# A two-layer model on one core: norms, FFN and query, key and value products in two halves of the tokens, a reordered mixer, and attention with rows stacked by four heads

## What is computed

```python
x = x + mamba2_mixer(layernorm(x))   # 32 heads of 64, state 128, 4 taps
x = x + ffn(layernorm(x))            # sigmoid(x w1) * (x w2), then w3; ternary weights, 704 wide
x = x + attention(layernorm(x))      # 16 heads of 16, causal, ALiBi
x = x + moe(layernorm(x))            # 64 experts, 6 per token, 64 slots each, and a shared expert
```

```python
attn = q @ k.T / sqrt(16) + slope * (j - i) + causal_mask
y = softmax(attn) @ v
```

## Time and profile before

| | |
|---|---|
| median of 3 runs | 1536.63 us (1531.63 to 1536.78) |
| the profiled execution: its own time | 1536.63 us |
| its span | 1534.8 us |
| TensorE busy | 1199.7 us, 78% |
| DVE busy | 909.1 us, 59% |
| ACT busy | 648.4 us, 42% |
| POOL busy | 584.1 us, 38% |
| DMA | 159.50 MB, mean 104 GB/s |

### The profile page before, as it was taken

How to read it: one execution, slowest core, us unless ns; L and a number is a source line. 1 busy time by engine, 2 the same in 40 slices (tenths; PEclk the granted TensorE clock), 3 DMA queues, 4 the chain that set the end, 5 groups by cost and what they waited for, 6 DMA issues and landing times.

```text
span 1534.8 us, 23644 instructions
## 1 busy us (share of the span) xinstructions
PE 1199.7 (78%) x8164; PEld 731.2 (48%) x8166; DVE 909.1 (59%) x1766; ACT 648.4 (42%) x1496; POOL 584.1 (38%) x789
## 2 busy tenths in 40 slices
PE   3799977778999876878999867779899775779950
PEld 2355544454555543555555534455555533555520
DVE  4577764446877744446977653456877643453426
ACT  3644423556444232546444224546544123431540
POOL 2255531210477712210577621110677611116660
PEclk9899988899999987998999987998999876989985
DMA  7455543400333235200333247001333529028779
GB/s 280 148 182 183 179 112 40 47 2 19 111 110 111 88 79 60 25 2 32 127 108 105 67 79 81 4 9 36 118 108 110 169 65 137 16 82 300 151 105 372
DMA packets 105957, 159.50 MB, mean 104 GB/s; under 512 B 10816, under 2 KB 67776, under 8 KB 105152
## 3 DMA queue, kind: packets, MB, share of 16 engines
q1 hardware_dynamic: 91056, 129.63, 33.1%
q0 software_dynamic: 9216, 19.98, 5.1%
q10 hardware_dynamic: 5568, 8.39, 1.5%
HBM read 104.55 MB, written 40.83 MB: 95 GB/s over the span
## 4 chain that ended last, share of the span: by engine, by line
PE 54%; DVE 14%; issue 9%; POOL 9%; ACT 6%; DMA 5%; ACTq 1%; SPq 1%; POOLq 0%; DVEq 0%
PE bank L1057 12%; PE bank L1099 5%; PE bank L982 5%; DMA joint<-pool_b 3%; PE bank L1163 3%; PE bank L1086 3%; PE bank L1078 3%; PE bank L1242 3%; DVE nmax L1668 2%; PE bank L1093 2%; DVE pool_c L1516 2%; PE bank L1184 2%; PE bank L1227 2%; DVE joint L1532 2%; PE bank L1315 2%
## 5 line engine op out<-in xcount | busy, mean ns | idle before, releaser
L1057 PE MATMUL bank<-xnT,joint 128*128 128x512 f32 x544 | 268.8, 618 | 3.4 <-ACT joint L745 1.7
L1959 POOL TENSOR_TENSOR joint<-joint 128x512 f32<-128x512 f32 x128 | 168.5, 1318 | 238.8 <-DVE joint L1532 237.6
L1516 DVE SCALAR_TENSOR_TENSOR pool_c<-bank,params,pool_c 128x511 f32<-128x511 f32 (+2 forms) x216 | 161.1, 747 | 81.1 <-ACT pool_c L706 75.7
L1668 DVE TENSOR_REDUCE nmax<-bank 128x1 f32<-128x512 f32 (+3 forms) x176 | 108.6, 638 | 112.3 <-PE bank L1204 111.2
L1057 PEld LDWEIGHTS bank<-xnT,joint 128*128 128x128 f32 x544 | 99.8, 197 | 101.8 <-issue 93.0
L982 PE MATMUL bank<-consts,pool_c 128*128 128x128 f32 (+1 forms) x368 | 69.5, 291 | 82.3 <-ACT pool_c L715 39.9
L848 ACT ACTIVATE pool_c<-bank 128x512 f32<-128x512 f32 (+1 forms) x176 | 95.0, 553 | 89.7 <-PE bank L1229 89.4
L1099 PE MATMUL bank<-wout,pool_c 128*128 128x256 f32 x512 | 127.0, 393 | 1.2 <-DVE pool_c L1557 1.2
L745 ACT ACTIVATE joint<-bank,dt_ 128x64 f32<-128x64 f32 x512 | 111.6, 338 | 13.0 <-PE bank L982 12.9
L1099 PEld LDWEIGHTS bank<-wout,pool_c 128*128 128x128 f32 x512 | 99.1, 197 | 34.3 <-issue 21.7
L731 ACT ACTIVATE pool_c<-bank 128x512 f32<-128x512 f32 x64 | 38.2, 598 | 175.6 <-PE bank L1057 175.6
(11 more groups left out here) (266 smaller groups left out, 2415.3 us busy)
## 6 DMA issues: line engine op xcount, KB each, us to landing
pool_b<-dA_rows SPq DMA_DIRECT2D x64, 256.0 KB
pool_b<-dec_rows SPq DMA_DIRECT2D x96, 128.0 KB
joint<-pool_b SPq DMA_DIRECT2D x48, 256.0 KB, 13.8
acc<-xrow SPq DMA_DIRECT2D x13, 640.0 KB, 5.3
joint<-dA_rows SPq DMA_DIRECT2D x32, 256.0 KB
dA_late<-dA_rows SPq DMA_DIRECT2D x32, 256.0 KB
xslot<-xrow SPq DMA_DIRECT2D x16, 321.0 KB, 4.5
pool_b<-xslot SPq DMA_DIRECT2D x64, 80.2 KB, 2.6
```

What stands on the lines that cost most here:

```text
L1057: last = mm(bank[:, :], win[:, k, col:col + P], xnT[:, k, :], start=(k == 0), stop=(k == KD - 1))
L1516: ins = v.scalar_tensor_tensor(out=cv[:, n:L], in0=bank[:, 0:L - n], scalar=convw[:, ci, TAPS - 1 - n:TAPS - n], in1=cv[:, n:L], op0=ALU.m ...
L1668: max_done.inc(v.tensor_reduce(nmax[:, t * AH + h0:t * AH + h0 + nh], src, AX.X, ALU.max, negate=True))
L1959: M_ready.inc(p.tensor_tensor(M[u % 2][:, hs_, :], Lx[:, hs_, :], cbm[:, c * P:(c + 1) * P].unsqueeze(1).to_broadcast([P, 4, P]), ALU.mult))
```

## The change

It has five parts.

1. `ffn`, its norms and `qkv` go over the tokens in two halves of 256. The six blocks of the first half come ahead of the six of the second; the low part of the first pair moves into `add_mixer(1)`, the second pair is turned at the fourth block. `add_ffn` and the next norm of tiles 0 and 1 stand inside the loop of the second half. The projections of the first half stand ahead of the turn of the second, and all row loads are waited for ahead of them.
2. Query and key columns are taken with a step of two (`w[:, k, e::2]`), so that a result holds the even or the odd heads, and each quarter of four heads lies in 64 partitions. SP moves the rows by quarters with four semaphores; `head_of` says which head a place in a quarter is. The loads of `rows` are two, and come last.
3. `AGROUPS` goes over the four tiles of quarter 0, then of quarter 1, then as before. "rows" stands at a group's middle. "copy" is a step of its own, right behind "values"; "turn" stays where it was.
4. In `mixer_steps` TensorE's first turn stands behind the unit's products, and ACT does tap, SiLU and skip term of a tile before it goes on to the next tile or gate.
5. The scatters start one step earlier; ACT's loading of the Exp table stands behind the copies of the coming norm.

```diff
-AGROUPS = [(t, q) for half in range(2) for t in range(T) for q in range(half * 2, half * 2 + 2)]
+AGROUPS = [(t, q) for q in range(2) for t in range(T)] + [(t, q) for t in range(T) for q in (2, 3)]
...
+        def head_of(q, h):
+            return q % 2 * (AH // 2) + 2 * h + q // 2
...
-                if i == min(1, turns - 1) and 1 <= g <= len(AGROUPS):
+                if i == turns // 2 and 1 <= g <= len(AGROUPS):
                     attention_steps.append(("rows", g - 1))
...
-            attention_steps.insert(min(i + 5, len(attention_steps)), ("turn", g))
+            attention_steps.insert(i + 1, ("copy", g))
+            attention_steps.insert(min(i + 6, len(attention_steps)), ("turn", g))
...
 # SP
                 for half in range(2):
                     sp.wait_ge(part3.sem, part3.upto(2 * half + 2, b))
-                    for i, (qp, kp) in enumerate(zip(QPARTS, KPARTS)):
-                        r0, kp = BROWS + i * AD, kp + 3
-                        stacked[half].inc(sp.dma_start(qks[r0:r0 + AD, half * 8:half * 8 + 8],
-                                                       parts[half][:, qp:kp + 1:kp - qp, :]))
+                    for q in (2 * half, 2 * half + 1):
+                        four = parts[half][q % 2 * (P // 2):(q % 2 + 1) * (P // 2)]
+                        for i, (qp, kp) in enumerate(zip(QPARTS, KPARTS)):
+                            r0, kp = BROWS + i * AD, kp + 3
+                            stacked[q].inc(sp.dma_start(qks[r0:r0 + AD, q * AQ:(q + 1) * AQ], four[:, qp:kp + 1:kp - qp, :]))
...
 # ACT, mixer_steps
                     for tile in early + late:
                         if tile[0] == "x":
                             tap(tile)
+                            silu(tile)
+                            skip_term(tile)
                         else:
                             gate(tile)
-                    for tile in early + late:
-                        if tile[0] == "x":
-                            silu(tile)
-                            skip_term(tile)
...
 # PE, mixer_steps
-                    for tile in first:
-                        turn_in(tile)
                     if s < UNITS:
                         within(s)
                         if s % T:
                             from_state(s)
+                    for tile in first:
+                        turn_in(tile)
...
 # PE, ffn
-                for p_ in range(2):
-                    norm_T(1, p_)
-                normed(1)
-                at(h_lo_done, 2)
-                for f in range(FT + 2):
-                    if f < FT:
+                norm_T(1, 0)
+                pe.wait_ge(ln_done.sem, ln_done.upto(pair_count(b, 1, 0)))
+                at(h_lo_done, 1)
+                for n in range(2 * FT + 2):
+                    p_, f = divmod(n, FT)
+                    if n == 3:
+                        norm_T(1, 1)
+                    if n == FT:
+                        normed(1)
+                        at(h_lo_done, 2)
+                    if n < 2 * FT:
...
+                    if n == 2 * FT:
+                        norm_T(2, 0)
...
 # PE, qkv
+                at(late_loaded, len(row_loads))
                 for p_ in range(2):
-                    norm_T(2, p_)
-                normed(2)
-                at(late_loaded, len(row_loads))
-                for m in range(4):
-                    half, w = m // 2, (wq, wk)[m % 2]
-                    for k in range(KD):
-                        last = mm(pb[2 + m][:, :], w[:, k, half * P:(half + 1) * P], xnT[:, k, :], start=(k == 0), stop=(k == KD - 1))
-                    qk_mm.inc(last)
+                    if p_ == 1:
+                        norm_T(2, 1)
+                    pe.wait_ge(ln_done.sem, ln_done.upto(pair_count(b, 2, p_)))
+                    cols = slice(p_ * 2 * P, (p_ + 1) * 2 * P)
+                    for m in range(4):
+                        e, w = m // 2, (wq, wk)[m % 2]
+                        for k in range(KD):
+                            last = mm(pb[2 + m][:, cols], w[:, k, e::2], xnT[:, k, cols], start=(k == 0), stop=(k == KD - 1))
+                        if p_ == 1:
+                            qk_mm.inc(last)
...
 # DVE, ffn
+                for n in range(2 * FT):
+                    p_, f = divmod(n, FT)
+                    if n == 3:
+                        low_part(1)
+                    if n == FT + 2:
+                        for t in range(2):
+                            add_ffn(t)
+                            norm_stats(2, t)
+                    if n == FT + 3:
+                        for t in range(2):
+                            norm_apply(2, t)
...
 # POOL, mixer_steps
-                    if done is not None and 1 <= s <= T * TOPK // 2:
+                    if done is not None and 0 <= s < T * TOPK // 2:
```

121 lines of the change are left out of this document (65 added, 56 removed).

## The result

The changed kernel takes **1400.29 us** (median of 4 runs, 1399.66 to 1403.28), the kernel before, beside it, 1534.13 (1531.37 to 1536.78): ratio 0.9132, 95% interval 0.9106 to 0.9157. The two profiled spans, 1534.8 and 1398.3, differ by 136.5 us, and those can be placed.

A forecast was written before the change was run, and what follows sets the result against it. The prediction saw no engine full and took TensorE's pauses as the bound. Mixer order 16, scatters 5, FFN and stacked rows 36.5 and attention 33 summed to 90.5 us off 1536.6, giving 1446 us, range 1408 to 1494.

The forecast's parts named there:

- 2 + 7.2: Stacked rows, last trip: about 2 us for DMAs to begin, then 7.2 for the first quarter's half of the bytes.
- that rival: Stacked rows: quarters move no faster than halves, so 11 us a trip come back, 1490 us; chance 0.08.
- all 32.7 us: Attention: copying outputs about five steps ahead removes all 32.7 us that TensorE's turn waits behind ACT.
- two thirds, 12 us: Attention: maxima rows moved to a group's middle remove two thirds of 17.9 us of waits, 12 us.
- 12 off for pairing: Attention: the new group order needs 63 loop turns instead of 58, charged 12 us for DVE's maxima.
- more comes off: Whole kernel: 39.9 us in the mixer, 48 in attention, 42 between, 5 scatters, 135 in all, 1401 us; chance 0.12.
- The last rest ends at 576.0: FFN in halves: its last step ends at 576.0 against 574.0 before, so the FFN itself loses 2 us.
- 1.35 us a step: FFN loop: DVE and ACT pace twelve half-width steps at 1.35 us each, where TensorE needs 1.30.
- 5.0 us of extras: FFN loop: added copy and low part 1.3, adds, statistics and norm 2.9, start at 1.2 GHz 0.8 us.
- The order: Mixer: TensorE's later turn and ACT's earlier SiLU remove one 1.30 us pause per group, 16 us in all.
- the scatters: Mixer: indirect DMAs one step earlier free POOL before its last products, 1.8 us in three trips, 5 us.

## Why the prediction was right or wrong

**Right.** The sign, and that waits of TensorE decide. In the mixer, that 40 us of waits behind ACT do not all go, as the turn then waits for DVE: 39.9 became 1.3, and 15.6 + 13.7 us of waits for the convolution stand against 8.7 + 1.2. A first FFN product 4.6 us earlier in trip 2 and 4.9 in the others (forecast 5.0). That the first quarter ends the wait only in the last trip: it waited 8.99 us there, forecast 2 + 7.2. Quarters do move faster, so that rival fell. Strided weights cost nothing that shows: their loads take 196 ns against 190 in the median.

**Wrong, attention: 64.6 instead of 33.** The prediction took "all 32.7 us" and "two thirds, 12 us", then 12 off for pairing. The first two were right in size when taken alone (the rows' wait fell by 12.3). Three terms failed. The charge for pairing was a wait for DVE's maximum that no run shows: the new order alone cost 11.8 us, all of it busy time at a lower clock, and with the rows moved it cost 0.8 to 1.8. The maxima's own waits fell from 7.0 to 0.7 us; they are not in the sum, though they stand on the same units. And busy time has no term in the sum. TensorE's over the four attentions fell from 234.2 to 216.2 us with the same products, 18.0 us. Trips 1 and 2 lost 2.7 each at nearly the same grant (0.94 and 0.93), trips 3 and 4 lost 5.1 and 7.5, where the grant went from 0.89 and 0.85 to 0.92. So part is the clock, and part seems to be products that follow one another where they followed a pause (the turn's take 278 ns instead of 308); how the two share it is not shown. 12 + 6.3 + 18.0 = 36 us against 31.6 missing; the rest fell short in the rows' wait, 7.3 instead of 12. The prediction's "more comes off" rival had 48 here and was still low.

**Wrong, the FFN and the rows: 46.2 instead of 36.5 up to the scores.** "The last rest ends at 576.0": in the same frame (the mixer's end at 547.0) it ended at 573.7. Its first gate product came at 554.9, where 554.8 was forecast, so the loop was mis-sized: 21.2 us from there on, measured 18.7. The sum charged DVE and ACT 1.35 us a step and 5.0 us of extras in series. The steps took 1.30, which is TensorE's pace, and only some 3 of the extras showed, most of them as waits of TensorE for DVE (1.34, 0.29, 0.65 and 0.21 us in trip 2). That is 2.3 us a trip, nearly all of the 10. The Trainium skill's "VectorE: DVE Perf Modes", section "The TRN2 errata — SBUF-src ops pay a fixed extra latency per instruction", advises tiles of 512 elements or more. The size of the cost agrees (gates 418 ns for half of 690, so 146 ns a split); following the advice cost 29.6 us here, since in most steps the loop does not wait for DVE, and the halves let each stage begin before the one ahead is done.

**Right in sum only, the mixer: 22.7 for 21.** The order was forecast at 16 us and gave 12 alone, the scatters at 5 and gave 13.7; together they share some of it. Inside the first, TensorE's order is worth more than forecast (5.7 to 6.0 us in every trip) and ACT's is a loss of 10.6; the prediction read ACT's order only for the SiLU that comes earlier, not for the tap that comes later behind it. For the scatters it priced the pause and not the clock behind it.

**Luck.** The rival "more comes off" ended at 1401 us and the kernel took 1400.29, but by other parts: it had 45 in mixer and scatters (measured 22.7), 42 between (46.2) and 48 in attention (64.6).

The fifth part's later load of the Exp table, the split of the row loads and the strided columns have no run of their own, so what each of them gives or costs is not shown.
